# Distance tables with the four batches side by side instead of as innermost index

## The chip, the cores and the metric

The program runs on one core of one Trainium2 chip. The metric is the time of one execution in microseconds of device time, lower is better. The kernel computes a small network of two blocks on 8 sequences of 512 tokens with 256 channels, in one launch; the change touches one stage of it, the first attention.

## The reference

Of the reference only the first attention matters here. It is an attention with 16 heads of 16 channels whose scores have two more terms, which depend on the distance between query and key:

```python
scores = jnp.einsum('bhqd,bhkd->bhqk', q, k) / scale
pos_k = (rel_embeddings @ Wk + bk).reshape(2 * ATT_SPAN, nH, d)      # 128 rows of distance buckets
c2p_att = jnp.einsum('bhqd,hpd->bhqp', q, pos_k)
c2p = jnp.take_along_axis(c2p_att, c2p_pos, axis=-1)                 # c2p_pos depends on q - k only
p2c_att = jnp.einsum('bhkd,hpd->bhkp', k, pos_k)
p2c = jnp.swapaxes(jnp.take_along_axis(p2c_att, p2c_pos, axis=-1), -1, -2)
scores = scores + (c2p + p2c) / scale
probs = jax.nn.softmax(scores, axis=-1)
ctx = jnp.einsum('bhqk,bhkd->bhqd', probs, v)
```

The bucket of a distance stops to change far from the diagonal, so that a row of c2p or p2c varies only in a band around the diagonal and is constant on either side of it.

## The kernel before

**Units.** The stage works in 128 units (`UNITS`): 16 heads, two groups of four batches each (`HB = 4`), and four tiles of 128 rows (`TPB = 4`, the tile is `t`). A unit is one tile of 128 query rows of one head, for four batches; inside a unit `j` counts the batches. `each_step` writes 16 units (`BODY`) into the body of a hardware loop, so the loop turns once every 16 units.

**Distance tables.** For each unit TensorE makes two tables in PSUM, of up to 320 columns (`TABLE`) per batch: table a from the queries (`table_a`, line 679) and table b from the keys (`table_b`, line 692). ScalarE copies all four batches of table a to `a_stage` (line 789); VectorE copies batches 0 and 2 of table b and ScalarE batches 1 and 3 to `b_stage` (`copy_b`, line 767). SyncE writes both stages to DRAM (`c2p_d`, line 591, and `p2c_d`, line 598). To turn "column is a distance" into "column is a key", the table is then read back with a skew: each row of DRAM is read from one element further left than the row above it. `read_skewed` (line 559) does that in four DMAs of 32 rows for each table and unit, into `c2p` (two buffers) and `p2c` (four, one per tile). GpSimd fills the constant columns beside the band (`fill`, line 629) from the table's end columns (`copy_ends`, line 655).

**Scores.** TensorE adds q times k and the transposed `p2c` in PSUM (`scores`, lines 706, 708, 711; `p2c` is the stationary operand, which is loaded as weights). VectorE adds `c2p`, takes the minimum of the negated row and writes `probs` (line 816), ScalarE takes the exponential (line 773), TensorE transposes (line 721), VectorE copies (line 825), and TensorE multiplies by v (line 734).

**Order.** Nothing is scheduled by a program: each engine's order is that of the code. In step i SyncE waits until the scores of unit i - 1 are made, issues the four reads of p2c for unit i + 2, the four reads of c2p for unit i + 1, every four units the loads of the next group of q and k (three DMAs of 384 KB), then the write of table a of unit i + 3 and the write of table b of unit i + 4. All of these go through one DMA queue in the order of issue. On TensorE the order within batch j is scores(j), table a(j) of unit i + 3, transposes(j) of unit i - 1, table b(j) of unit i + 4; after j = 1 the product with v of unit i - 2. The single bank of table b makes TensorE wait at `table_b` until the copy of the batch before has left it.

**Layout before.** All stage buffers, DRAM tables and read tiles have the batch as innermost index, for example `a_stage[P, 2, TABLE, HB]`. A copy of one batch therefore writes every fourth float (a step of 16 bytes), VectorE's read of `c2p[:, slot, :, j]` and TensorE's weight load from `p2c` have the same step, and a row of the skewed read is one run of up to 288 x 4 floats, 4608 bytes.

Of the kernel before, what the change touches and what calls it, by code (L numbers as in the profile page):

```python
# [14 lines left out]
P = 128  # L15
# [42 lines left out]
def build(nc, a, out, taps=None):  # L58
# [8 lines left out]
    with whole:  # L67
# [33 lines left out]
        c2p_d = dram("c2p_d", [4, P, TABLE, B // 2], F32)  # L101
        p2c_d = dram("p2c_d", [4, P, TABLE, B // 2], F32)
# [349 lines left out]
        def table_cols(t):  # L452

            return (ROWS, TABLE) if t == 0 else (0, TABLE - ROWS) if t == TPB - 1 else (0, TABLE)

# [23 lines left out]
        with ExitStack() as st:  # L479
# [58 lines left out]
            with nc.Block() as block:  # L538
                @block.sync
                def _(sp):  # L540
# [13 lines left out]
                    def read_skewed(table_d, slot, t, dest, left, done):  # L554
                        for g in range(P // ROWS):
                            j0, j1 = varied(t, g)
                            skew = bass.AP(table_d.tensor, ((slot * P + ROWS * g) * TABLE + ROWS - 1 - ROWS * g + j0) * HB,
                                           [[(TABLE - 1) * HB, ROWS], [1, (j1 - j0) * HB]])
                            sp.dma_start(dest[g * ROWS:(g + 1) * ROWS, j0 + left:j1 + left, :].rearrange("p n b -> p (n b)"),
                                         skew).then_inc(done, 16)  # L560

                    def step(i, w):
# [25 lines left out]
                        if is_unit(ia, wa):  # L588
                            sp.wait_ge(a_copied, HB * (BODY * ia + wa) + HB)
                            x0, x1 = table_cols(wa % TPB)  # L590
                            sp.dma_start(c2p_d[wa % 4, :, x0:x1, :].rearrange("p n b -> p (n b)"),
                                         a_stage[:, wa % 2, x0:x1, :].rearrange("p n b -> p (n b)")).then_inc(a_written[wa % 2], 16)
                        if is_unit(ib, wb):
# [3 lines left out]
                            x0, x1 = table_cols(wb % TPB)  # L597
                            sp.dma_start(p2c_d[wb % 4, :, x0:x1, :].rearrange("p n b -> p (n b)"),
                                         b_stage[:, wb % 2, x0:x1, :].rearrange("p n b -> p (n b)")).then_inc(b_written[wb % 2], 16)
# [16 lines left out]
                def _(pool):  # L616
# [3 lines left out]
                    def step(i, w):  # L620
# [7 lines left out]
                        def fill(dest, ends_of, side, c0, c1):  # L628
                            return pool.tensor_copy(dest[:, c0:c1, :], ends_of[:, side, :].unsqueeze(1).broadcast_to(  # L629
                                [P, c1 - c0, HB]))  # L630
# [1447 lines left out]
```

## Time and profile before

| | |
|---|---|
| time before | 2948.34 us, median of 3 runs (2947.35 to 2954.58) |
| the profiled execution | 2920.05 us; its span 2918.4 us |
| the stage of the change | about 292 us to 1517 us of the span, 128 units |
| busy in the span | TensorE 1966.0 us, VectorE 1921.8 us, ScalarE 1234.3 us, GpSimd 939.9 us |
| DMA in the span | 492.63 MB, 208344 packets |

The profile gives for each engine the time in which it is busy, for each group of instructions its count, its mean time and what ended the idle time before it, and for the DMA engines how much of the time of the core's 16 engines packets were under way, with the rate in GB/s. The profiled execution took 1.65 us more than its span, and 28 us less than the median of the runs without a profile; sums are made against the profiled one, and differences are carried over to the median.

### The profile page before, as it was taken

How to read it: one execution, taken by the hardware profiler on the slowest of the kernel's cores; microseconds unless marked ns; L12 is line 12 of the kernel's file. 1: busy time of each engine (PE TensorE's matmuls, PEld its weight loads, DVE VectorE, ACT ScalarE, POOL GpSimd, SP SyncE). 2: the span in 40 equal slices, each digit the busy share in tenths (PEclk: the TensorE clock that was granted, in tenths of full speed). 3: DMA queues.
4: the chain of work that ended last, by engine and by line, in shares of the span. 5: the costliest groups of instructions: out<-in, count | busy, mean ns of one | idle time of the engine just before them, and what ended most of it. 6: DMA issues, size and time to landing. Idle time of an engine off the chain costs nothing. (4 is left out here: it accounts for less than half of the span.)

```text
span 2918.4 us, 47884 instructions
## 1 busy us (share of the span) xinstructions
PE 1966.0 (67%) x13524; PEld 1442.7 (49%) x13525; DVE 1921.8 (66%) x4329; ACT 1234.3 (42%) x2141; POOL 939.9 (32%) x1177
## 2 busy tenths in 40 slices
PE   4452677777777777777763888867613515999963
PEld 2231466555565655566552656644312502888631
DVE  5652688777787878788874666618774775444454
ACT  2332666666666666666640232224300115333200
POOL 3222222222222222222222221114774001555576
PEclk8776799999999999899986999988756555999986
DMA  4666988888888989889964121000000141444644
GB/s 136 210 204 179 292 274 284 269 275 276 265 287 273 288 271 291 267 273 289 294 184 110 43 58 29 0 20 0 0 0 2 59 165 40 154 155 151 126 131 124
DMA packets 208344, 492.63 MB, mean 169 GB/s; under 512 B 39169, under 2 KB 104353, under 8 KB 208129
## 3 DMA queue, kind: packets, MB, share of 16 engines
q1 hardware_dynamic: 179392, 420.25, 45.5%
q0 software_dynamic: 24576, 57.11, 7.9%
q10 hardware_dynamic: 4160, 12.58, 1.1%
q8 instruction: 112, 1.84, 0.3%
q14 instruction: 104, 0.84, 0.1%
HBM read 248.45 MB, written 241.30 MB: 168 GB/s over the span
## 5 line engine op out<-in xcount | busy, mean ns | idle before, releaser
L816 DVE CUSTOM_DVE_ANT_0 probs<-bank,c2p 128x512 f32<-128x512 f32 x512 | 551.5, 1077 | 231.8 <-PE bank L711 154.5
L789 ACT COPY a_stage<-bank 128x320 f32<-128x320 f32 (+1 forms) x512 | 364.5, 712 | 275.2 <-PE bank L679 269.2
L773 ACT ACTIVATE probs<-probs,neg_max 128x512 f32<-128x512 f32 x512 | 363.6, 710 | 22.5 <-DVE neg_max L816 22.0
L692 PE MATMUL bank<-tab,k 96*128 96x320 bf16 (+1 forms) x512 | 160.8, 314 | 286.1 <-DVE b_stage L767 227.8
L825 DVE COPY probsT<-bank 128x512 f32<-128x512 f32 x512 | 351.6, 687 | 2.5 <-PE bank L721 2.5
L721 PE MATMUL bank<-ident,probs 128*128 128x128 f32 x2048 | 326.5, 284 | 4.1 <-ACT probs L773 3.9
L721 PEld LDWEIGHTS bank<-ident,probs 128*128 128x128 f32 x2048 | 261.4, 148 | 18.4 <-issue 6.2
L711 PE MATMUL bank<-ident,p2c 128*128 128x128 f32 x1280 | 263.9, 307 | 0.0
L2017 POOL DMA_INDIRECT p_x_tile<-y_d,p_token x160 | 152.5, 953 | 328.2 <-POOLq L1708 208.2
L655 POOL COPY end_c2p<-a_stage 128x4 f32<-128x4 f32 (+1 forms) x128 | 24.1, 188 | 721.3 <-ACT a_stage L789 571.6
L767 ACT COPY b_stage<-bank 128x288 f32<-128x288 f32 (+1 forms) x256 | 186.3, 728 | 151.9 <-PE bank L692 150.9
L692 PEld LDWEIGHTS bank<-tab,k 96*128 96x128 bf16 x512 | 50.8, 99 | 353.3 <-DVE b_stage L767 287.7
L706 PE MATMUL bank<-k,q 96*128 96x384 bf16 (+1 forms) x512 | 162.8, 318 | 76.3 <-DMA p2c<-p2c_d 46.7
L711 PEld LDWEIGHTS bank<-ident,p2c 128*128 128x128 f32 x1280 | 199.5, 208 | 24.3 <-issue 5.6
L767 DVE COPY b_stage<-bank 128x288 f32<-128x288 f32 (+1 forms) x256 | 177.4, 693 | 47.9 <-PE bank L692 47.9
L629 POOL COPY c2p<-end_c2p 128x1408 f32<-128x1408 f32 (+2 forms) x192 | 175.4, 933 | 7.2 <-DVE neg_max L816 7.2
L1883 PE MATMUL bank<-p_w_all,p_xT 128*128 x640 | 170.7, 390 | 1.0 <-issue 0.9
L1212 POOL TENSOR_TENSOR p_pv<-p_v,p_score 128x1024 f32<-128x1024 f32 (+1 forms) x32 | 144.0, 4532 | 69.3 <-DVE p_attn L1390 48.4
L679 PE MATMUL bank<-tab,q 96*128 96x320 bf16 (+1 forms) x512 | 160.5, 314 | 1.5 <-ACT a_stage L789 0.8
L734 PE MATMUL bank<-probsT,v_h 128*32 128x128 f32 x4096 | 154.8, 297 | 0.8 <-DVE probsT L825 0.8
L1960 DVE TENSOR_TENSOR p_h<-bank,p_e_silu 128x128 f32<-128x128 f32 x160 | 46.7, 292 | 150.5 <-ACT p_e_silu L1942 150.5
L2026 POOL DMA_INDIRECT p_w_all<-o_sorted_d,p_slot x128 | 122.9, 960 | 52.4 <-issue 35.7
(252 smaller groups left out, 3931.3 us busy)
## 6 DMA issues: line engine op xcount, KB each, us to landing
p2c_d<-b_stage SPq DMA_DIRECT2D x64, 640.0 KB, 3.6
c2p_d<-a_stage SPq DMA_DIRECT2D x64, 640.0 KB, 3.4
p2c_d<-b_stage SPq DMA_DIRECT2D x64, 576.0 KB, 7.8
c2p_d<-a_stage SPq DMA_DIRECT2D x64, 576.0 KB, 5.8
p2c<-p2c_d SPq DMA_DIRECT2D x256, 144.0 KB
c2p<-c2p_d SPq DMA_DIRECT2D x256, 144.0 KB, 5.9
o_sorted_d<-p_o_pair SPq DMA_DIRECT2D x80, 256.0 KB, 2.3
q_stack_d<-p_parts SPq DMA_DIRECT2D x96, 128.0 KB
```

The source lines that it names most:

```text
L629: return pool.tensor_copy(dest[:, c0:c1, :], ends_of[:, side, :].unsqueeze(1).broadcast_to([P, c1 - c0, HB]))
L679: pe.matmul(bank[A_BANK][:, x0:x1], q6[:, g, 0, j * S + t * P:j * S + (t + 1) * P], tab6[:, w // 8, 0, x0:x1], start=True, stop=True).then ...
L692: pe.matmul(bank[B_BANK][:, x0:x1], k6[:, g, j * S + t * P:j * S + (t + 1) * P], tab6[:, w // 8, 1, x0:x1], start=True, stop=True).then_in ...
L706: pe.matmul(sc[:, near], q6[:, g, 0, own], k6[:, g, j * S + lo * P:j * S + (hi + 1) * P], start=True, stop=False, skip_group_check=True)
L711: last = pe.matmul(sc[:, kt * P:(kt + 1) * P], p2c[:, kt, (t - kt + 1) * P:(t - kt + 2) * P, j], ident[:], start=False, stop=kt == hi, is_ ...
L721: last = pe.transpose(bank[T_BANKS[j % 2]][:, kt * P:(kt + 1) * P], probs[:, w % 2, j, kt * P:(kt + 1) * P], ident[:])
L767: copy(b_stage[:, w % 2, x0:x1, j], bank[B_BANK][:, x0:x1]).then_inc(copied, 1)
L773: act.activation(probs[:, w % 2, j, :], probs[:, w % 2, j, :], ACT.Exp, bias=neg_max[:, w % 2, j:j + 1], scale=-1.0).then_inc(exp_done, 1)
L789: act.copy(a_stage[:, wa % 2, x0:x1, j], bank[A_BANK][:, x0:x1]).then_inc(a_copied, 1)
L816: dve.tensor_tensor_reduce(probs[:, w % 2, j, :], bank[S_BANKS[(HB * w + j) % 3]][:], c2p[:, w % 2, :, j], -SCALE, LOWEST, ALU.add, ALU.mi ...
L825: dve.tensor_copy(probsT[:, wp % 2, j], bank[T_BANKS[j % 2]][:].rearrange("p (k q) -> p k q", k=TPB)).then_inc(probsT_copied, 1)
L1883: last = pe.matmul(bank[GU_BANKS[w % 2]][:, 0:2 * INNER], xT[:, w % 2, c, :], weights(of_round[w], 2 * c * INNER, 2 * (c + 1) * INNER), st ...
```

## The change

The batch moves from innermost to second index in the two stage buffers, in both DRAM tables and in both read tiles. With it the columns 0 to 31 and 288 to 319, which the first and the last tile of a sequence did not make, copy or write, are now made, copied and written for all tiles (`table_cols` is gone), because the written block would otherwise not be one run per partition.

```diff
-        c2p_d = dram("c2p_d", [4, P, TABLE, B // 2], F32)
-        p2c_d = dram("p2c_d", [4, P, TABLE, B // 2], F32)
+        c2p_d = dram("c2p_d", [4, P, B // 2, TABLE], F32)
+        p2c_d = dram("p2c_d", [4, P, B // 2, TABLE], F32)
...
-        def table_cols(t):
-
-            return (ROWS, TABLE) if t == 0 else (0, TABLE - ROWS) if t == TPB - 1 else (0, TABLE)
...
-            a_stage = sb(st, "a_stage", [P, 2, TABLE, HB])
-            b_stage = sb(st, "b_stage", [P, 2, TABLE, HB])
-            c2p = sb(st, "c2p", [P, 2, S, HB])
+            a_stage = sb(st, "a_stage", [P, 2, HB, TABLE])
+            b_stage = sb(st, "b_stage", [P, 2, HB, TABLE])
+            c2p = sb(st, "c2p", [P, 2, HB, S])
...
-            p2c = sb(st, "p2c", [P, TPB, NEAR, HB])
+            p2c = sb(st, "p2c", [P, TPB, HB, NEAR])
...
-                            skew = bass.AP(table_d.tensor, ((slot * P + ROWS * g) * TABLE + ROWS - 1 - ROWS * g + j0) * HB,
-                                           [[(TABLE - 1) * HB, ROWS], [1, (j1 - j0) * HB]])
-                            sp.dma_start(dest[g * ROWS:(g + 1) * ROWS, j0 + left:j1 + left, :].rearrange("p n b -> p (n b)"),
-                                         skew).then_inc(done, 16)
+                            skew = bass.AP(table_d.tensor, (slot * P + ROWS * g) * HB * TABLE + ROWS - 1 - ROWS * g + j0,
+                                           [[HB * TABLE - 1, ROWS], [TABLE, HB], [1, j1 - j0]])
+                            sp.dma_start(dest[g * ROWS:(g + 1) * ROWS, :, j0 + left:j1 + left], skew).then_inc(done, 16)
...
-                            x0, x1 = table_cols(wa % TPB)
-                            sp.dma_start(c2p_d[wa % 4, :, x0:x1, :].rearrange("p n b -> p (n b)"),
-                                         a_stage[:, wa % 2, x0:x1, :].rearrange("p n b -> p (n b)")).then_inc(a_written[wa % 2], 16)
+                            sp.dma_start(c2p_d[wa % 4], a_stage[:, wa % 2]).then_inc(a_written[wa % 2], 16)
...
-                    copy(b_stage[:, w % 2, x0:x1, j], bank[B_BANK][:, x0:x1]).then_inc(copied, 1)
+                    copy(b_stage[:, w % 2, j, :], bank[B_BANK][:, 0:TABLE]).then_inc(copied, 1)
...
-                                act.copy(a_stage[:, wa % 2, x0:x1, j], bank[A_BANK][:, x0:x1]).then_inc(a_copied, 1)
+                                act.copy(a_stage[:, wa % 2, j, :], bank[A_BANK][:, 0:TABLE]).then_inc(a_copied, 1)
...
-                                    probs[:, w % 2, j, :], bank[S_BANKS[(HB * w + j) % 3]][:], c2p[:, w % 2, :, j],
+                                    probs[:, w % 2, j, :], bank[S_BANKS[(HB * w + j) % 3]][:], c2p[:, w % 2, j, :],
```

No instruction is added, removed or moved; the counts per engine stay, only shapes change. On SyncE's queue in the loop's body, the reads of p2c for tile 1 or 2, the reads of c2p for tile 3, and the writes around them stand before as

```order
L559 DMA p2c<-p2c_d 32x1152 x4
L559 DMA c2p<-c2p_d 32x640
L559 DMA c2p<-c2p_d 32x768
L559 DMA c2p<-c2p_d 32x896
L559 DMA c2p<-c2p_d 32x1024
L591 DMA c2p_d<-a_stage 128x1280
L598 DMA p2c_d<-b_stage 128x1152
```

and after the change as

```order
L555 DMA p2c<-p2c_d 32x4x288 x4
L555 DMA c2p<-c2p_d 32x4x160
L555 DMA c2p<-c2p_d 32x4x192
L555 DMA c2p<-c2p_d 32x4x224
L555 DMA c2p<-c2p_d 32x4x256
L585 DMA c2p_d<-a_stage 128x1280
L590 DMA p2c_d<-b_stage 128x1280
```

A row of a skewed read is now four runs of up to 288 floats instead of one run of up to 1152; a write is still one run of 1280 floats per partition, for all tiles.

## Rows read from the trace of the kernel before

**Rows 1.** The whole stage in one window: columns, then busy time of each engine
```profile
core 0: us, PE busy (x) PEld busy (x) DVE busy (x) ACT busy (x) POOL busy (x), PEclk, DMA share, GB/s
300.00:1500.00 1200.00, 888.42 (x9296) 711.71 (x9296) 962.36 (x1763) 795.49 (x1289) 310.92 (x646) 0.93 0.88 278
```

**Rows 2.** The instructions on probs: line 816, times, first and last start
```profile
L816 DVE CUSTOM_DVE_ANT_0 probs<-bank,c2p x512: 1005/1079/1180, 306.0 to 1508.2; 128x512 f32<-128x512 f32 x171
```

**Rows 3.** Waits from 300 to 1500 us: who waited for whom, us, times, longest
```profile
PE bank L692 <- DVE b_stage L767: 224.9, 227, 2.8
DVE probs L816 <- PE bank L711: 154.5, 140, 5.3
DVE probs L816 <- DMA c2p<-c2p_d: 69.7, 51, 5.3
PE bank L706 <- DMA p2c<-p2c_d: 46.7, 37, 3.1
PE bank L706 <- issue: 27.3, 9, 5.3
```

**Rows 4.** DMA from 700 to 740 us in 40 slices of 1 us: busy tenths, rate
```profile
DMA  9999999999999700008999899899999999999899
GB/s 376 423 402 310 252 229 235 373 417 413 402 318 237 182 22 0 0 0 324 389 404 299 247 256 230 213 401 400 397 313 258 238 221 215 274 262 262 221 362 414
```

**Rows 5.** SyncE's DMA issues between 708 and 722 us: start, us, issue
```profile
708.41 1.73 SPq L559 DMA_DIRECT2D c2p<-c2p_d  x4
717.40 0.34 SPq L591 DMA_DIRECT2D c2p_d<-a_stage  x1
718.61 0.34 SPq L598 DMA_DIRECT2D p2c_d<-b_stage  x1
719.82 2.48 SPq L559 DMA_DIRECT2D p2c<-p2c_d  x4
```

**Rows 6.** DMA issues of the tables: KB each, median us to landing
```profile
c2p_d<-a_stage SPq DMA_DIRECT2D x64, 576.0 KB, 5.8
c2p<-c2p_d SPq DMA_DIRECT2D x256, 144.0 KB, 5.9
```

**Rows 7.** The page's groups: busy us, mean ns of one, idle before
```profile
L816 DVE CUSTOM_DVE_ANT_0 probs<-bank,c2p 128x512 f32<-128x512 f32 x512 | 551.5, 1077 | 231.8 <-PE bank L711 154.5
L789 ACT COPY a_stage<-bank 128x320 f32<-128x320 f32 (+1 forms) x512 | 364.5, 712 | 275.2 <-PE bank L679 269.2
L767 DVE COPY b_stage<-bank 128x288 f32<-128x288 f32 (+1 forms) x256 | 177.4, 693 | 47.9 <-PE bank L692 47.9
L825 DVE COPY probsT<-bank 128x512 f32<-128x512 f32 x512 | 351.6, 687 | 2.5 <-PE bank L721 2.5
```

**Rows 8.** Groups by shape outside the stage, same columns
```profile
L1972 DVE COPY p_o_pair<-bank 128x256 f32<-128x256 f32 x160 | 66.7, 417 | 1.1 <-PE bank L1895 0.8
L1937 ACT COPY p_xT<-bank 128x256 f32<-128x256 f32 x160 | 59.5, 372 | 88.7 <-PE bank L1876 88.5
L1307 ACT COPY p_qk<-bank 128x512 f32<-128x512 f32 x32 | 18.7, 585 | 51.5 <-PE bank L1248 49.1 <-DVE p_score L1366 2.4
L1052 DVE TENSOR_TENSOR p_o<-bank,p_n_bo 128x512 f32<-128x512 f32 x16 | 11.1, 692 | 44.4 <-PE bank L961 44.4
L1596 DVE TENSOR_TENSOR p_picked<-p_hit,p_rank_e 128x4096 f32<-128x4096 f32 x1 | 7.1, 7102 | 0.0
L1574 DVE TENSOR_TENSOR p_picked<-p_hit,p_score 128x4096 f32<-128x4096 f32 x1 | 4.4, 4399 | 0.0
```

**Rows 9.** DMA from 3 to 4 us, input rows of 1 KB read from DRAM
```profile
DMA packets 367, 0.37 MB, mean 373 GB/s; under 512 B 3, under 2 KB 367, under 8 KB 367
```

**Rows 10.** SyncE's issue of a DMA, ns, min/median/max: table reads, input reads, a 3-level write
```profile
L559 SPq DMA_DIRECT2D c2p<-c2p_d x512: 302/421/1778, 301.0 to 1499.2; - x171
L903 SPq DMA_DIRECT2D p_x<-in_x x8: 387/414/1106, 1536.6 to 1775.6; - x8
L220 SPq DMA_DIRECT2D q_stack_d<-p_parts x96: 603/625/1816, 48.7 to 251.8; - x96
```

More of the change, by code:

```diff
@@ L596, in step @@
                             sp.wait_ge(b_copied_act, 2 * (BODY * ib + wb) + 2)
[L597 to L599 removed]
+                            sp.dma_start(p2c_d[wb % 4], b_stage[:, wb % 2]).then_inc(b_written[wb % 2], 16)
                         ic, wc = ahead(i, w, -2)
@@ L628, in fill @@
                         def fill(dest, ends_of, side, c0, c1):
-                            return pool.tensor_copy(dest[:, c0:c1, :], ends_of[:, side, :].unsqueeze(1).broadcast_to(
-                                [P, c1 - c0, HB]))
+                            return pool.tensor_copy(dest[:, :, c0:c1], ends_of[:, side, :].unsqueeze(2).broadcast_to(
+                                [P, HB, c1 - c0]))
                         if is_unit(i2, w2):
@@ L654, in copy_ends @@
                             apart(pool)
-                            pool.tensor_copy(ends_of[:, w % 4, ends(t), :], stage[:, w % 2, end_cols(t), :]
-                                             ).then_inc(copied, 1)
+                            pool.tensor_copy(ends_of[:, w % 4, ends(t), :].rearrange("p s b -> p b s"),
+                                             stage[:, w % 2, :, end_cols(t)]).then_inc(copied, 1)
                         if is_unit(ia, wa):
@@ L677, in table_a @@
                         wait_count(pe, a_copied, HB * m + j)
-                        x0, x1 = table_cols(t)
-                        pe.matmul(bank[A_BANK][:, x0:x1], q6[:, g, 0, j * S + t * P:j * S + (t + 1) * P],
-                                  tab6[:, w // 8, 0, x0:x1], start=True, stop=True).then_inc(a_made, 1)
+                        pe.matmul(bank[A_BANK][:, 0:TABLE], q6[:, g, 0, j * S + t * P:j * S + (t + 1) * P],
+                                  tab6[:, w // 8, 0, :], start=True, stop=True).then_inc(a_made, 1)
                     def table_b(i, w, j):
@@ L690, in table_b @@
                             wait_count(pe, b_copied_act, 2 * m + j // 2)
-                        x0, x1 = table_cols(t)
-                        pe.matmul(bank[B_BANK][:, x0:x1], k6[:, g, j * S + t * P:j * S + (t + 1) * P],
-                                  tab6[:, w // 8, 1, x0:x1], start=True, stop=True).then_inc(b_made, 1)
+                        pe.matmul(bank[B_BANK][:, 0:TABLE], k6[:, g, j * S + t * P:j * S + (t + 1) * P],
+                                  tab6[:, w // 8, 1, :], start=True, stop=True).then_inc(b_made, 1)
                     def scores(i, w, j):
@@ L710, in scores @@
                         for kt in range(lo, hi + 1):
-                            last = pe.matmul(sc[:, kt * P:(kt + 1) * P], p2c[:, kt, (t - kt + 1) * P:(t - kt + 2) * P, j],
+                            last = pe.matmul(sc[:, kt * P:(kt + 1) * P], p2c[:, kt, j, (t - kt + 1) * P:(t - kt + 2) * P],
                                              ident[:], start=False, stop=kt == hi, is_transpose=True,
```

2 lines of the change are left out of this document (removed).

## The prediction

> **What bounds the kernel now.** I first read the stage as one window [rows 1]. From 300 to 1500 us VectorE is busy 962.36 of 1200 us (80%), TensorE 888.42, ScalarE 795.49, and the DMA engines have packets under way 0.88 of the time. No engine is full; the DMA share is the highest number in the row. The instructions on probs give the length of a unit: 512 instructions of line 816 start from 306.0 to 1508.2 us, so four of them, one unit, take 4 x 1202.2 / 511 = 9.41 us [rows 2]. With [rows 1], in a unit VectorE works 0.802 x 9.41 = 7.55 us, TensorE 6.97 us, ScalarE 6.24 us, the DMA engines 0.88 x 9.41 = 8.28 us; they are idle for 1.13 us.
>
> Then the waits [rows 3]. Two kinds take turns. TensorE waits 224.9 us for VectorE's copy of table b, and VectorE 154.5 us for TensorE's scores: the two hand work to and fro, and a faster VectorE shortens both. But VectorE also waits 69.7 us for the skewed read of c2p, at 51 of 128 units, and TensorE 46.7 us for that of p2c at 37. So in a good part of the units the read is late, not the arithmetic.
>
> Last the DMA by microsecond [rows 4]. The reader is to see three levels. Near 400 to 420 GB/s the tables are written; at 213 to 258 GB/s, with the same 9 tenths busy, the skewed reads run; and for 715 to 717 us nothing runs. The issues tell which is which [rows 5]: the reads issued at 708.41 us are through by 714; the write of table a is issued at 717.40 us; with the write of table b it makes the slices of 324 to 404; the reads from 719.82 us make those of 299 down to 213. The hole from 714 to 718 us is the time in which SyncE waits until ScalarE has copied table a of that unit. So the DMA queue has work for 8.28 us per unit, and idles when the arithmetic is late with a copy; the arithmetic idles when a read lands late behind the loads of q and k. A read of c2p takes 5.9 us from issue to landing [rows 6].
>
> **What the change gives the engines.** VectorE's line 816 reads c2p with a step of 16 bytes and takes 1077 ns [rows 7]. What such a step costs is shown outside the stage: of two instructions of the same operation and size, the one whose second operand has a large step takes 7102 ns and the one without 4399 ns for 4096 elements, 0.66 ns per element [rows 8]. For 512 that is 338 ns, so line 816 falls to about 739 ns. A plain tensor_tensor of 512 from PSUM takes 692 ns [rows 8], so both estimates agree. If line 816's length were its own and not the step's, this gain would be 0; the 692 ns make me take the 338.
>
> The copy of table b takes 693 ns on VectorE [rows 7]. Copies without a step take 417 ns for 256 columns [rows 8] and 687 ns for 512 [rows 7], 1.055 ns per column, so 484 ns for 320 columns, which all tiles now have: 209 ns less. Per unit VectorE saves 4 x 338 + 2 x 209 = 1770 ns, and has 5.78 us of work. ScalarE's copies take 712 ns [rows 7]; without a step 372 ns for 256 and 585 ns for 512 [rows 8] give 425 ns for 320. Six per unit save 1.7 us. ScalarE was never waited for long; this matters since SyncE's write of table a stands behind it. TensorE's weight loads from p2c lose their step too; they lie beside matmuls, and I count 0. Its table matmuls get 32 more columns in half of the units; TensorE's 6.97 us leave 2.4 us of cover, and without it this would be a tenth of those matmuls in those units.
>
> The Trainium skill, SBUF — State Buffer, Specifications, says that SBUF is read in lines of 16 bytes and that an access which goes to a new line each time pays. A step of four floats is just that, and the rows above agree.
>
> GpSimd's fills write as many elements as before and its copies of end columns are tiny; I take 0 for both, and they are covered by the issue of the p2c reads ahead of the c2p reads.
>
> **What it costs the DMA queue.** Writes: tiles 0 and 3 wrote 576 KB per table [rows 6] and now write 128 x 1280 floats, 640 KB, on average 64 KB more per unit; at about 400 GB/s [rows 4] this is 0.16 us. Reads: same bytes, but each of the 256 rows of a unit's eight reads comes in 4 runs of at most 1152 bytes, 768 more pieces. The trace has no such read. The nearest row is that of input rows of 1 KB read from DRAM: 373 GB/s, 43.9 ns for a piece on one of 16 engines [rows 9]. At the best rate of large pieces, 423 GB/s [rows 4], the same bytes take 38.7 ns, so a piece has 5.2 ns of its own, and 768 of them on 16 engines cost 0.25 us per unit. That is the upper bound. The lower bound is 0, and I lean to it: the skewed reads now run at 213 to 258 GB/s, far below the 373 that pieces of 1 KB reach, so something other than the piece limits them, and the piece's overhead can hide under it. A gain I exclude, since bytes, rows and partitions stay. I take 0.10 us. SyncE's issue of one read has a median of 421 ns; a load with four runs per partition has 414, a write with three levels and a register in its address 625 [rows 10]. I take no change; at 625 it would be 8 x 0.204 = 1.6 us more per unit on a queue that issues for about 4.2 us of 9.4.
>
> The Trainium skill, SBUF — State Buffer, Door 1, says that 32 partitions reach only 8 of the 16 ports, 218 GB/s; each skewed read fills 32 partitions, and the slices of 213 to 258 agree with that. The Trainium skill, DMA: Bandwidth & Descriptors, How a descriptor splits into AXI transactions, speaks against the change: a piece that does not start on a multiple of 256 bytes fetches up to 256 bytes more. By that page, as an estimate, 768 pieces fetch up to 197 KB more, which at 240 GB/s would be 0.8 us per unit.
>
> **The sum.** The arithmetic can now do a unit in less than the queue: VectorE 5.78 us, TensorE 6.97 us with waits around it. So the unit is what the queue needs, plus what idling stays. Need: 8.28 + 0.16 + 0.10 = 8.54 us. Idle before: 1.13 us. Of it a part does not go: at the turn of the hardware loop TensorE stands up to 5.3 us, 27.3 us in all [rows 3], 0.21 us per unit. Of the other 0.92 us I keep a third, 0.30, for the latency between a read's landing and the next write. The unit is 8.54 + 0.21 + 0.30 = 9.05 us, 0.36 us less; times 128 units 46 us. Against the profiled 2920.05 us that gives 2874; carried to the median of the runs, 2948 - 46 = 2902 us.
>
> The forecast's own range: with nothing for pieces and no idle but that of the loop turns, the unit is 8.28 + 0.16 + 0.21 = 8.65 us, 97 us less, 2851. With 0.25 us for pieces and half of the 0.92 us of idle kept it is 8.28 + 0.16 + 0.25 + 0.21 + 0.46 = 9.36 us, 6 us less, 2942.
>
> **Rivals.**
> Slower: the queue's need grows by more than its idling shrinks. The place is the skewed reads. It decides from the point where growth plus remaining idle passes 1.13 us. If pieces cost 0.25 us and the arithmetic, since it has only two buffers for c2p, can't issue its writes earlier, the unit is 8.28 + 0.41 + 1.13 = 9.82 us, 52 us more, 3001. For it speaks that the queue is already at 0.88; against it that the hole from 714 to 718 us [rows 4, 5] ends with the issue of a write that had waited for a copy, and that copy gets faster. Chance 0.12. By the Trainium skill's rule on pieces off 256 bytes, named above, the same rival would come by another road: 8.28 + 0.16 + 0.8 + 0.51 = 9.75 us, an estimate of 2992 us; no row here shows that cost, and it shares the 0.12.
>
> No change: either line 816 keeps its 1077 ns (VectorE then works 7.13 us, most of the idle stays, and the unit is about 9.4 us) or cost and gain cancel. 2939 to 2957. Chance 0.12.
>
> Much faster: the busy share of the DMA engines is no need, but packets that wait and would go faster if asked earlier. Then the hand-over between VectorE and TensorE was the bound, and the unit falls to TensorE's 6.97 us and some 0.6 us of waits, 7.6 us: 232 us less, 2716; halfway, 2830. For it speaks that 154.5 + 224.9 us of waits hang on VectorE. Against it: 16 engines are busy at 213 to 258 GB/s [rows 4], and c2p lands late at 51 units already. Chance 0.10.
>
> The forecast itself has 0.66.
>
> **How the numbers follow.** Faster by over 0.3% (about what a measurement of this kernel can tell from no change, 9 us): the forecast and the last rival, 0.76. Within 0.3%: 0.12. Slower: 0.12. The range that holds 8 in 10 covers the forecast and no change, and a little of each side: 2845 to 2960.
>
> **What would show it.** Line 816 near 740 ns and the copies of tables near 484 (VectorE) and 425 ns (ScalarE) would show the first step. VectorE's wait for c2p should grow from 69.7 us at more than 51 units, its wait for TensorE and TensorE's for the b copy should shrink, and the DMA share of the window should rise to 0.93 or more. The slices of the reads should stay at 213 to 258 GB/s; if they fall below 200, the pieces cost what I leaned against, and I am wrong on the slow side. If the share falls with a shorter unit, I am wrong on the fast side.

## The result, and the profile after

The changed kernel takes 2924.62 us (median of 6 runs, 2918.56 to 2938.00), the kernel before 2947.85 us in the same sets of runs. The ratio is 0.9926, with an interval of 0.9898 to 0.9954: 22 us faster, where 46 were forecast. The time lies in the forecast's range, and the gain is a little under half of the forecast gain.

The length of the stage and of a unit, in the trace of the changed kernel (line 803 is line 816 of before; times are minimum, median and maximum in ns, then first and last start in us):

```profile
L803 DVE CUSTOM_DVE_ANT_0 probs<-bank,c2p x512: 679/691/694, 301.4 to 1483.8; 128x512 f32<-128x512 f32 x171
```

A unit is 4 x 1182.4 / 511 = 9.256 us where it was 9.41 [rows 2]: 0.155 us less, 20 us over 128 units. In these two traces the stage also starts 4.6 us earlier, and it ends 24.4 us earlier; the start is not the change's doing, for in a second trace of the kernel before (e16) it lies at 302.9 us. The medians differ by 23 us, about what the stage gained. The last section says why the profiled times of the two kernels (2920.05 and 2926.19 us) do not show it.

The page's groups after, as in [rows 7] (busy us, mean ns, idle before):

```profile
L803 DVE CUSTOM_DVE_ANT_0 probs<-bank,c2p 128x512 f32<-128x512 f32 x512 | 351.5, 687 | 423.4 <-PE bank L700 215.3
L776 ACT COPY a_stage<-bank 128x320 f32<-128x320 f32 x512 | 217.8, 425 | 490.0 <-PE bank L669 444.0
L755 DVE COPY b_stage<-bank 128x320 f32<-128x320 f32 x256 | 123.2, 481 | 47.4 <-PE bank L681 47.4
```

The engine terms came as forecast or better: 687 ns (forecast 739), 425 (425) and 481 (484). The window of [rows 1] after the change:

```profile
300.00:1500.00 1200.00, 916.22 (x9443) 734.19 (x9442) 752.29 (x1785) 644.03 (x1294) 314.63 (x650) 0.88 0.93 285
```

VectorE fell from 962 to 752 us and ScalarE from 795 to 644, and the share of the DMA engines rose from 0.88 to 0.93. TensorE's mean granted clock fell from 0.93 to 0.88: of its two levels, 1.2 and 2.4 GHz, it had the lower one for 24% of the window instead of 14%. Its work per unit rose from 6.97 to 7.07 us. The waits, as in [rows 3]:

```profile
DVE probs L803 <- PE bank L700: 215.3, 172, 7.5
DVE probs L803 <- DMA c2p<-c2p_d: 188.3, 65, 7.3
PE bank L695 <- DMA p2c<-p2c_d: 138.2, 52, 5.0
PE bank L681 <- DVE b_stage L755: 79.5, 129, 2.9
PE bank L695 <- issue: 36.8, 10, 7.2
```

The time that VectorE no longer works has become waiting. Waits for the two reads grew from 116.4 us (69.7 + 46.7) to 326.5 us (188.3 + 138.2). TensorE's wait for the b copy fell from 224.9 to 79.5 us, but VectorE's wait for the scores rose from 154.5 to 215.3 us. TensorE's longer wait for p2c explains little of that: laid side by side in the trace, the two waits overlap in 13 us. For most of it TensorE was at work, and VectorE, whose operations are shorter, stood waiting for it. The DMA slices from 700 to 740 us, as in [rows 4]:

```profile
DMA  9815999999999999999999999999999999999955
GB/s 266 192 31 246 410 400 248 303 251 230 251 345 423 420 326 249 232 243 240 215 266 242 250 214 391 415 421 348 245 241 249 337 408 430 387 316 252 238 125 231
```

The holes are nearly gone. The levels are the old ones: writes at 400 to 430 GB/s, reads at 214 to 266. The read of c2p lands later after its issue, 6.8 us against 5.9 [rows 6]:

```profile
c2p<-c2p_d SPq DMA_DIRECT2D x256, 144.0 KB, 6.8
```

### The profile page after: what moved, and what is told of

Its sections match the earlier page's. It is cut to its first block and busy times, and to the rows that moved or that the text cites. A ratio compares the mean times of both kernels' runs of the same rounds, so it can differ in the third digit from the quotient of the medians.

```text
span 2924.5 us, 47884 instructions
## 1 busy us (share of the span) xinstructions
PE 1980.1 (68%) x13524; PEld 1454.9 (50%) x13525; DVE 1695.2 (58%) x4329; ACT 1072.3 (37%) x2141; POOL 941.1 (32%) x1177
## 5 line engine op out<-in xcount | busy, mean ns | idle before, releaser
L803 DVE CUSTOM_DVE_ANT_0 probs<-bank,c2p 128x512 f32<-128x512 f32 x512 | 351.5, 687 | 423.4 <-PE bank L700 215.3
L776 ACT COPY a_stage<-bank 128x320 f32<-128x320 f32 x512 | 217.8, 425 | 490.0 <-PE bank L669 444.0
L710 PE MATMUL bank<-ident,probs 128*128 128x128 f32 x2048 | 346.9, 297 | 1.4 <-ACT probs L761 1.2
L710 PEld LDWEIGHTS bank<-ident,probs 128*128 128x128 f32 x2048 | 288.6, 156 | 16.5 <-issue 2.6
L681 PE MATMUL bank<-tab,k 96*128 96x320 bf16 x512 | 171.5, 335 | 146.8 <-DVE b_stage L755 82.3
L700 PEld LDWEIGHTS bank<-ident,p2c 128*128 128x128 f32 x1280 | 163.2, 156 | 26.6 <-issue 7.6
L669 PE MATMUL bank<-tab,q 96*128 96x320 bf16 x512 | 171.8, 336 | 0.0
L695 PEld LDWEIGHTS bank<-k,q 96*128 96x128 bf16 x512 | 52.4, 102 | 226.1 <-issue 183.2
L755 DVE COPY b_stage<-bank 128x320 f32<-128x320 f32 x256 | 123.2, 481 | 47.4 <-PE bank L681 47.4
L697 PE MATMUL bank<-k,q 96*128 96x128 bf16 (+1 forms) x512 | 136.0, 266 | 0.0
```

The lines of the kernel that those rows point to most:

```text
L669: pe.matmul(bank[A_BANK][:, 0:TABLE], q6[:, g, 0, j * S + t * P:j * S + (t + 1) * P], tab6[:, w // 8, 0, :], start=True, stop=True).then_i ...
L681: pe.matmul(bank[B_BANK][:, 0:TABLE], k6[:, g, j * S + t * P:j * S + (t + 1) * P], tab6[:, w // 8, 1, :], start=True, stop=True).then_inc( ...
L695: pe.matmul(sc[:, near], q6[:, g, 0, own], k6[:, g, j * S + lo * P:j * S + (hi + 1) * P], start=True, stop=False, skip_group_check=True)
L700: last = pe.matmul(sc[:, kt * P:(kt + 1) * P], p2c[:, kt, j, (t - kt + 1) * P:(t - kt + 2) * P], ident[:], start=False, stop=kt == hi, is_ ...
L710: last = pe.transpose(bank[T_BANKS[j % 2]][:, kt * P:(kt + 1) * P], probs[:, w % 2, j, kt * P:(kt + 1) * P], ident[:])
L776: act.copy(a_stage[:, wa % 2, j, :], bank[A_BANK][:, 0:TABLE]).then_inc(a_copied, 1)
```

## The experiments

The unit of each kernel is worked out as above, from the first and the last start in its trace. Ratios are to the kernel before, run on the same chip. A unit comes from one profiled execution, and that execution can lie off the median of its kernel: 21 us below for e10, 6 to 7 below for e9 and e11, 11 above for e6 and e8, 13 above for e18. In a unit this is 0.05 to 0.16 us, so a difference of units of 0.1 us counts only where the ratios say the same.

| | edit | unit us | ratio (interval) |
|---|---|---|---|
| | before / before again (e16) | 9.41 / 9.42 | 1 |
| | changed kernel | 9.26 | 0.993 (0.990 to 0.995) |
| e1 | before, contiguous engine operations | 8.95 | 0.981 (0.978 to 0.983) |
| e2 | before, reads cut, negative step | 9.68 | 1.013 (1.010 to 1.015) |
| e3 | e1 and e2 | 9.30 | 0.996 (0.994 to 0.998) |
| e4 | changed, writes at 288 columns in 4 runs | 9.25 | 0.994 (0.992 to 0.996) |
| e5 | e1, reads cut, positive step | 9.05 | 0.982 (0.979 to 0.985) |
| e6 | changed, row starts on 16 bytes | 9.32 | 0.993 (0.990 to 0.995) |
| e7 | e1, row starts on any 4 bytes | 8.99 | 0.981 (0.978 to 0.984) |
| e8 | changed, reads of distant halves in turn | 9.12 | 0.982 (0.980 to 0.985) |
| e9 | e1, 320 columns everywhere | 9.16 | 0.990 (0.987 to 0.993) |
| e10 | changed, reads in pairs 1, 0, 3, 2 | 9.13 | 0.993 (0.991 to 0.996) |
| e11 | changed, e8 and e13 together | 8.84 | 0.976 (0.973 to 0.979) |
| e12 | before, reads as in e8 | 9.27 | 0.992 (0.990 to 0.994) |
| e13 | changed, 288 columns in one run | 9.07 | 0.984 (0.983 to 0.986) |
| e14 | changed, reads half as long | 8.50 | 0.961 (0.959 to 0.963) |
| e15 | before, reads half as long | 8.84 | 0.975 (0.973 to 0.977) |
| e17 | changed, loads in three steps | 9.17 | 0.988 (0.985 to 0.991) |
| e18 | e11 and e17 | 8.94 | 0.974 (0.970 to 0.978) |

**e1, the engines alone.** Copies, line 816 and the weight loads walk flat rows; all DMAs are those of before.

```diff
-                    copy(b_stage[:, w % 2, x0:x1, j], bank[B_BANK][:, x0:x1]).then_inc(copied, 1)
+                    flat = b_stage[:, w % 2].rearrange("p n b -> p (n b)")
+                    at = HB * x0 + j * (x1 - x0)
+                    copy(flat[:, at:at + x1 - x0], bank[B_BANK][:, x0:x1]).then_inc(copied, 1)
```

> The kernel before, with its tiles, DMAs and column counts, but every engine operation on the stage buffers and on the read tile walks them contiguously instead of at a step of four. It reads and writes the tables in another order, so the values of the distance terms are not the reference's. It asks what the shorter engine times alone are worth. Theory (the queues' work bounds the unit): DVE's weighted sum near 690 ns instead of 1077, the unit 8.28 of DMA need + 0.21 of loop turns + 0.3 to 0.5 of kept idle = 8.8 to 9.0 us instead of 9.41, so 50 to 80 us less than before, about 2880. Rival (the hand-over between engines bounds it): 7.6 us per unit, over 200 us less. Second rival (engine times were never on the path): the unit stays at 9.4 and the time at 2948.

The instructions of line 816, which is line 825 here, and the window from 300 to 1400 us, which lies wholly in the stage:

```profile
L825 DVE CUSTOM_DVE_ANT_0 probs<-bank,c2p x512: 678/690/693, 299.6 to 1442.6; 128x512 f32<-128x512 f32 x171
```

```profile
300.00:1400.00 1100.00, 865.67 (x8927) 694.71 (x8925) 705.47 (x1698) 603.78 (x1244) 297.49 (x620) 0.88 0.94 293
```

62 us less and a unit of 8.95 us: the first theory. The shorter operations are worth 0.46 us of a unit, and the other parts of the change take two thirds of that back. (In e1 the granted clock is 0.88 too, so it did not fall by those other parts.)

**e2 and e3, the reads in four pieces.**

```diff
-                                            [[(TABLE - 1) * HB, ROWS], [1, (j1 - j0) * HB]])
+                                            [[(TABLE - 1) * HB, ROWS], [-n, HB], [1, n]])
```

The read begins 3 * n floats on, and its target steps back in the same way.

> The kernel before, in which each skewed read of a table comes in four pieces a quarter as long, with the same bytes and the same layout; all that is computed stays. It asks what the smaller pieces of the change cost by themselves. Theory: 768 extra pieces per unit cost 0 to 0.25 us, so the unit is 9.4 to 9.66 us and the time 0 to 32 us more. Rival: the pieces cost much more, 0.8 us per unit and 100 us in all, and are what ate the gain of the change. Second rival: the DMA need isn't what bounds, and the time stays within 5 us.

> The two edits together: contiguous engine operations and reads in four pieces, without the 32 extra columns per batch that the change writes. It reads and writes the tables in another order, so the values of the distance terms are not the reference's. Theory: the unit of the first experiment plus 0.1 to 0.25 us for the pieces, 8.95 to 9.2 us, which is the changed kernel's 9.26 less up to 0.16 for the narrower writes; time 2900 to 2925. Rival (pieces are cheap, the writes are the loss): the same time as the first experiment within 5 us.

Both lost, a little more than the theories allow: 0.27 us of a unit on before, 0.36 on e1. But the edit brought something that the change does not have. SyncE's issue of a read in e2 (min, median, max ns):

```profile
L563 SPq DMA_DIRECT2D c2p<-c2p_d x512: 560/601/1752, 300.1 to 1533.1; - x171
```

601 ns, where before has 421 [rows 10] and the changed kernel 432. Eight reads per unit make 1.4 us more on SyncE's queue. So neither run prices the pieces, and e5 does it again with a positive step.

**e4, the writes narrower.**

```diff
-                            sp.dma_start(c2p_d[wa % 4], a_stage[:, wa % 2]).then_inc(a_written[wa % 2], 16)
+                            x0, x1 = table_cols(wa % TPB)
+                            sp.dma_start(c2p_d[wa % 4, :, :, x0:x1], a_stage[:, wa % 2, :, x0:x1]).then_inc(a_written[wa % 2], 16)
```

> The changed kernel, with the first and the last stage buffer of a row written out at 288 columns of each batch instead of 320 (four runs of 1152 bytes per partition instead of one of 5120); all that is computed stays. It asks what the wider writes cost. Theory: they are 0.16 us per unit, so the unit falls from 9.26 to 9.1 us and the time by 20 us, to about 2904. Rival (a write costs by its count of pieces and not by its bytes): the time stays at 2924 or rises by a few us.

No gain. The rival seemed to hold, that columns cost nothing. But this edit too trades one thing for another: it cuts each of these writes into four runs of 1152 bytes. e9 and e13 price the columns without that, but they change more than the write: the columns are also made and copied, or not.

**e5, e6 and e7: count and place of the pieces.**

e5, on e1:

```diff
-                                            [[(TABLE - 1) * HB, ROWS], [1, (j1 - j0) * HB]])
+                                            [[(TABLE - 1) * HB, ROWS], [j1 - j0 - 4, HB], [1, j1 - j0]])
```

e6, on the changed kernel (all reads also begin at column 124, so that the rows stay inside the table):

```diff
-                                           [[HB * TABLE - 1, ROWS], [TABLE, HB], [1, j1 - j0]])
+                                           [[HB * TABLE - 4, ROWS], [TABLE, HB], [1, j1 - j0]])
```

e7, on e1:

```diff
-                                            [[(TABLE - 1) * HB, ROWS], [1, (j1 - j0) * HB]])
+                                            [[(TABLE - 1) * HB + 1, ROWS], [1, (j1 - j0) * HB]])
```

> The first experiment's kernel (contiguous engine operations, values of the distance terms not the reference's), with each skewed read in four pieces that overlap by four floats at their source, so that a piece keeps its place on 16 bytes and SP issues the read at a positive step. Experiments 2 and 3 cut the reads with a negative step, and SP took 601 ns to issue one instead of 421, which may be their loss. Theory A (the count of pieces costs, on the queues): SP's issue near 430 ns, and still the unit is 8.95 + 0.30 = 9.25 us as in the changed kernel, the time 38 us over the first experiment, 2924. Theory B (the loss of experiments 2 and 3 was SP's issue time, and what the changed kernel lost was the place of its row starts): the time of the first experiment within 8 us, 2886.

> The changed kernel, in which the rows of a skewed read begin four floats apart instead of one, all on multiples of 16 bytes as in the kernel before; counts and sizes of pieces stay. It reads other columns of the tables, so the values of the distance terms are not the reference's. Theory A (the count of pieces costs): no change, 2924 within 8 us. Theory B (row starts at any 4 bytes cost): the unit falls from 9.26 towards 8.95 us and the time to about 2886.

> The first experiment's kernel with long pieces of 4608 bytes as there, whose rows begin one float off from row to row, at any multiple of 4 bytes (values of the distance terms not the reference's). Theory A (count of pieces): the first experiment's time, 2886 within 8 us. Theory B (place of row starts): a loss; a quarter as many starts as in the changed kernel, so 8 to 38 us over it.

SyncE's issue of a c2p read in e5:

```profile
L559 SPq DMA_DIRECT2D c2p<-c2p_d x512: 302/432/1966, 297.0 to 1449.7; - x171
```

Its median is 432 ns, as in the changed kernel. The stage of e5 ends 15 us after that of e1:

```profile
L825 DVE CUSTOM_DVE_ANT_0 probs<-bank,c2p x512: 679/688/694, 302.5 to 1458.0; 128x512 f32<-128x512 f32 x171
```

The 768 extra pieces of a unit cost 0.10 us of it by these two profiles; the ratios (0.982 against 0.981) give 0.03 us, and do not tell it from nothing. Theory A of e5, 38 us for the pieces, falls. Where the rows start, on 16 bytes or on any 4, makes no difference that can be seen: e6 equals the changed kernel by its ratio, e7 equals e1. So the second half of theory B, that the change lost by its row starts, falls too; its first half, that the issue time was the loss of e2 and e3, is left standing, though the direction of their step differs too. Most of the 0.31 us between e1 and the changed kernel had to be something else.

**e9 and e13, the 32 columns.** e9 lets all of e1's tables be 320 wide, and e13 makes the changed kernel's first and last table of a row 288 wide, packed side by side.

e9, on e1:

```diff
-            return (ROWS, TABLE) if t == 0 else (0, TABLE - ROWS) if t == TPB - 1 else (0, TABLE)
+            return (0, TABLE)
```

e13, on the changed kernel:

```diff
+        def packed(rows, t):
+            x0, x1 = table_cols(t)
+            return rows[:, 0:HB * (x1 - x0)]
...
-                            sp.dma_start(c2p_d[wa % 4], a_stage[:, wa % 2]).then_inc(a_written[wa % 2], 16)
+                            sp.dma_start(packed(c2p_d[wa % 4], wa % TPB), packed(a_stage[:, wa % 2], wa % TPB)).then_inc(a_written[wa % 2], 16)
```

> The first experiment's kernel (contiguous engine operations, long pieces, values of the distance terms not the reference's), with all 320 columns of each batch computed, copied and written for every stage buffer, as the changed kernel does. It adds the columns alone. Theory (the columns cost what the forecast's write term says, 0.16 us per unit): the unit goes from 8.95 to 9.11 us, and with the 0.10 that cutting the reads was measured at this makes 9.2 of the changed kernel's 9.26; time 20 us over the first experiment, 2906. Rival (the columns cost nothing, as the fourth experiment suggests, and where the pieces of a read land is what costs): the first experiment's time within 8 us.

> The changed kernel with the batches of the first and the last table of a row side by side at 288 columns instead of 320, computed, copied and written as such in one piece of 4608 bytes per partition; the order of the reads is the changed kernel's. All that is computed stays. Theory (the 32 columns cost 0.22 us per unit, as between experiments 1 and 9): the unit falls from 9.26 to 9.04 us, the time by 28 us, ratio to the kernel before 0.983. Rival (the columns cost nothing, as experiment 4 seems to say): ratio 0.993.

The stage of e9:

```profile
L825 DVE CUSTOM_DVE_ANT_0 probs<-bank,c2p x512: 679/691/694, 300.3 to 1471.0; 128x512 f32<-128x512 f32 x171
```

The stage of e13 (its line 822 is line 803 of the changed kernel):

```profile
L822 DVE CUSTOM_DVE_ANT_0 probs<-bank,c2p x512: 678/690/693, 301.4 to 1459.7; 128x512 f32<-128x512 f32 x171
```

The columns cost 9.16 - 8.95 = 0.22 us (with unrounded units) on e1, and taking them out of the changed kernel gives back 9.26 - 9.07 = 0.19 us, with ratios 0.009 apart, some 25 us. These are columns that TensorE makes, the engines copy and SyncE writes; how much of the price is the written bytes, neither run separates. e4 took away the written bytes alone and had no gain. That its four runs ate one is likely but not shown: its queues have a share of 0.97, against 0.95 in the changed kernel and in e13, though they move 7 GB/s less than the changed kernel's.

**e8, e10 and e12, the order of a table's four reads.**

```diff
-                        for g in range(P // ROWS):
+                        for g in (0, 2, 1, 3):
```

(e10 has (1, 0, 3, 2).)

> The changed kernel, in which SP issues the four reads of a table for partitions 0 to 31, 64 to 95, 32 to 63, 96 to 127 instead of in rising order; all that is computed stays. Theory (while two reads are in the queues together they are bound by the part of the memory that 32 or 64 neighbouring partitions reach; 213 to 258 GB/s in the read phases): reads of distant partitions run side by side, the reads' phase shortens by a tenth or more, the unit falls by 0.2 to 0.5 us and the time by 25 to 60 us. Rival (the level comes from the order in which each queue works off its pieces, or from the pieces themselves): 2924 within 8 us.

> The changed kernel, in which SP issues the four reads of a table for partitions 32 to 63, 0 to 31, 96 to 127, 64 to 95: another order than the rising one, but neighbours still follow each other in the same half. All that is computed stays. Theory (experiment 8's gain came from reads of different halves in the queues together): no gain, 2924 within 8 us, unit 9.26. Rival (any order that breaks the rising one gains, by the sizes of the reads or the part of DRAM they start in): about 2900, unit 9.12.

> The kernel before with the order of experiment 8 alone (partitions 0 to 31, 64 to 95, 32 to 63, 96 to 127). All that is computed stays. Theory (the read phases bound the kernel before too): a gain of the same size, 0.1 to 0.3 us of the unit's 9.41, 15 to 35 us, about 2925. Rival (before, the engines' waits keep most of it, since its idle share was 0.12 against 0.07): less than 8 us.

Order 0, 2, 1, 3 takes 1.0% off the changed kernel and 0.8% off the kernel before; order 1, 0, 3, 2 takes nothing by its ratio, 0.993. (Its unit of 9.13 is that of a run 21 us below the median.) So it is not a new order as such that gains, but one in which reads of partitions 64 apart follow each other. The queues' work shows it as well: from 300 to 1500 us the share is 0.89 in e8 and 0.94 in e10, with units of the same length and the same bytes. The Trainium skill, SBUF — State Buffer, Door 1, has a reason: partitions 32 apart share the DMA ports, partitions 64 apart have others. The trace agrees in the landing of a c2p read, 5.5 us against 6.8:

```profile
c2p<-c2p_d SPq DMA_DIRECT2D x240, 144.0 KB, 5.5
```

e11 puts e8 and e13 together. Its theory was that the gains add, 2881 to 2901 us where the kernel before takes 2948, a ratio of 0.977 to 0.984. It has 0.976, so they do.

**e14 and e15, half of each read.**

```diff
                             j0, j1 = varied(t, g)
+                            j1 = (j0 + j1) // 2
```

> The changed kernel with only the first half of the columns of each skewed read (pieces of 320 to 576 bytes, as many as before; the rest of the read tiles is zero, so the values of the distance terms are not the reference's). Theory (the queues' work bounds the unit): 8.6 us of work per unit falls by some 2 us, to 6.4 to 6.6, and the unit falls to the hand-over bound of the prediction's last rival, 7.6 us, or with kept idle of 0.65 even to 7.1; over 190 us less than the changed kernel, below 2740. Rival (the unit is held by the engines' chain and the queues only look full): 9.0 to 9.3 us, less than 30 us gained.

> The kernel before with only the first half of the columns of each skewed read (the rest of the read tiles is zero, so the values of the distance terms are not the reference's). Theory (the kernel before is bound by the queues with engines close behind): the unit falls to where the longer engine operations bound it, by DVE's 962 of 1200 us of work 7.6 us at the least and with its idle time by the chain near 8.4 us; 2820 or less. What it is over the run before (with the changed kernel's shorter operations) is what these are worth with the queues out of the way: 0.7 us per unit or more, against the 0.46 of experiment 1. Rival: both fall to the same unit.

The unit falls, but to 8.50 us: not to the theory's 7.1 or 7.6, and below the rival's 9.0 to 9.3. Four units in turn of e14, each from the first instruction of line 806 (803 of the changed kernel) to that of the next unit; columns as in [rows 1]:

```profile
644.85:652.09 7.24, 5.26 (x67) 4.39 (x68) 5.82 (x14) 4.23 (x10) 1.74 (x5) 1.00 0.85 266
652.09:663.56 11.47, 6.71 (x73) 5.20 (x72) 5.81 (x14) 4.79 (x10) 4.01 (x7) 0.83 0.98 323
663.56:671.56 8.00, 7.89 (x79) 6.54 (x78) 6.01 (x15) 5.05 (x11) 0.27 (x2) 0.82 0.52 163
671.56:678.84 7.28, 6.41 (x76) 5.16 (x75) 5.81 (x16) 5.12 (x11) 3.34 (x8) 1.00 0.84 277
```

Three of four units take 7.2 to 8.0 us with the queues at 0.52 to 0.85. The other one takes 11.5 with the queues full: before it, from 649.8 to 652.2 us, SyncE has issued the next group of k and q, and here the next head's tables too, ahead of the writes and reads that follow. In the changed kernel:

```profile
676.05:684.33 8.28, 7.32 (x84) 5.91 (x81) 5.82 (x15) 5.86 (x12) 1.96 (x5) 1.00 1.04 280
684.33:696.99 12.66, 7.60 (x73) 6.08 (x73) 5.91 (x15) 5.10 (x11) 2.96 (x6) 0.87 1.05 321
696.99:703.74 6.75, 5.55 (x70) 4.50 (x69) 5.73 (x14) 4.16 (x10) 0.26 (x2) 1.00 0.81 264
703.74:712.89 9.15, 6.39 (x76) 5.15 (x75) 5.81 (x16) 5.10 (x11) 4.97 (x10) 1.00 1.03 319
```

(A share counts the packets that began in the stretch with all their time, so in a single unit it can pass 1.) Both bounds are there, in different units, and a mean unit hides it. The whole stage says the same. With the units sorted into their four kinds, in the order of these lines, and each kind's mean length taken from the starts on probs (units 5 to 124 of the 128), the kernel before has 9.37, 10.50, 8.80 and 9.29 us, the changed kernel 8.80, 11.15, 7.66 and 9.78, and e14 8.05, 10.32, 7.70 and 8.29; the second trace of before (e16) differs from the first by 0.12 at most, that of e6 from the changed kernel's by 0.25. So the change shortened two kinds of units, by 0.57 and 1.14 us, and lengthened the other two, by 0.65 and 0.49: two thirds of the gain came back as longer units, and these are the kinds whose queues are full above.

e15 is 0.34 us over e14, and not the 0.7 or more expected. This is the price of the whole layout, its pieces and columns included, and not that of the operations alone: with half of each read the change is worth 0.34 us of a unit, with whole reads 0.155.

**e17 and e18, the loads spread.**

```diff
-                        if w % TPB == 0 and is_unit(i, w) and is_unit(*ahead(i, w, 2 * TPB)):
-                            load_group(2 * i + w // 8 + 1, (w // TPB) % 2, (w // TPB + 2) % 4)
+                        if w % TPB < 3 and is_unit(i, w) and is_unit(*ahead(i, w - w % TPB, 2 * TPB)):
+                            load_group(2 * i + w // 8 + 1, (w // TPB) % 2, (w // TPB + 2) % 4, [w % TPB])
```

> The changed kernel, in which SP issues the three loads of the next k and q group in three steps (k in the first unit of a row, q in the second, the far q in the third) instead of all three in the first. Bytes and all that is computed stay. Theory (the unit with the loads holds 2 to 3 us that the others can't take back): the unit of 11.5 us falls to 9.5 to 10.5 while two others rise by 0.3 to 0.6, the mean falls by 0.1 to 0.4 us and the time by 15 to 50 us, ratio to before 0.975 to 0.988. Rival (the queues' work sets the mean whatever its order): ratio 0.993 as the changed kernel's.

> Experiment 11's kernel (tables at 288 columns side by side, reads issued by distant halves) with the loads in three steps as in experiment 17. All that is computed stays. Theory: as much below experiment 11's ratio of 0.976 as experiment 17 is below the changed kernel's 0.993, 0.960 to 0.972. Rival: 0.976.

Four units in turn of e17; the load of k is issued ahead of the second, at 675.2 us, and that of q in it, at 683.3 us:

```profile
671.34:679.50 8.16, 7.54 (x86) 6.23 (x84) 5.82 (x15) 6.10 (x13) 1.85 (x5) 1.00 1.04 265
679.50:689.85 10.35, 8.26 (x78) 6.49 (x76) 6.00 (x15) 5.49 (x12) 2.55 (x6) 0.84 1.06 312
689.85:698.77 8.92, 7.16 (x70) 5.98 (x71) 6.00 (x14) 4.29 (x9) 1.30 (x4) 0.81 1.05 301
698.77:707.05 8.28, 6.07 (x73) 4.85 (x72) 5.82 (x14) 4.96 (x11) 3.80 (x9) 1.00 1.01 328
```

The long unit shrank and its neighbour grew, from 6.75 to 8.92 us (over the stage, in the mean, 11.15 to 9.41 and 7.66 to 8.65); the queues are now full in all four. The mean fell by 0.09 us. The ratio, 0.988, is at the edge of the theory's window, its interval overlaps that of the changed kernel, and e18 is not told apart from e11. So the loads in one place are not what holds most of the time. That with them spread the sum of the queues' work does fits the full queues, but was not tried by itself. e11 and e18 beat both kernels; e11's ratio, 0.976, with its interval, is the surer of the two.

**e16, the kernel before again.**

> The kernel before, unchanged, for its profile. The stage of the tables ended at 1508 us in the first profile, and everything after it took 1410 us. If the chip sets the latter, it is 1410 where the median of before is near 2921 and 1437 to 1443 where it is near 2948, while the stage ends at 1505 to 1511 on both. If the first profile was only a lucky run, the later code takes about 1440 here whatever the median.

Line 816 in its trace:

```profile
L816 DVE CUSTOM_DVE_ANT_0 probs<-bank,c2p x512: 1005/1079/1156, 302.9 to 1506.7; 128x512 f32<-128x512 f32 x171
```

Its span is 2954.6 us, on a chip where the kernel before has a median of 2951.28: the stage ends as in [rows 2], and the rest takes 1448 us, not 1410.

## Why the prediction came out at half

- **That the DMA queues bound the changed kernel, and arithmetic that gets shorter shows only in part:** right. VectorE's busy time per unit fell by 1.75 us (7.55 to 0.627 x 9.256 = 5.80), and the unit by 0.155.
- **The engine durations:** right for the copies; line 816 was priced 52 ns too long, since the step cost it 0.76 ns per element and not 0.66. The sum does not use it, since it takes the unit to be what the queues need.
- **"Need: 8.28 + 0.16 + 0.10 = 8.54 us":** this is the step that failed. It takes what the queues did before, 8.28 us, as a fixed amount that other work is added to. Windows that lie wholly in the stage, of the changed kernel, e9, e5, e4 and e14 in turn:

```profile
300.00:1400.00 1100.00, 844.74 (x8596) 676.43 (x8595) 686.74 (x1638) 594.43 (x1202) 288.65 (x600) 0.87 0.95 290
300.00:1400.00 1100.00, 847.07 (x8660) 675.85 (x8659) 690.51 (x1651) 599.44 (x1211) 290.13 (x604) 0.88 0.93 293
300.00:1400.00 1100.00, 852.53 (x8800) 683.89 (x8800) 695.87 (x1674) 597.73 (x1228) 292.92 (x610) 0.88 0.95 289
300.00:1400.00 1100.00, 834.83 (x8592) 667.75 (x8590) 685.50 (x1637) 595.94 (x1202) 289.00 (x600) 0.89 0.97 283
300.00:1380.00 1080.00, 864.30 (x9274) 693.31 (x9277) 734.86 (x1760) 635.64 (x1285) 310.49 (x641) 0.92 0.79 256
```

The changed kernel's queues work 0.95 x 9.26 = 8.79 us of a unit, 0.25 more than the sum has, and idle for 0.46 us, where the sum kept 0.51. So the 0.21 us by which the unit was missed lie in the need. With the bytes and the pieces of before, e1 already has 0.94 x 8.95 = 8.41 us for what made 8.28. On top of it the cut reads add 0.95 x 9.05 - 8.41 = 0.18 us and the columns 0.93 x 9.16 - 8.41 = 0.11 (shares are rounded, which leaves 0.05 us in each of these).
- **"Of the other 0.92 us I keep a third, 0.30":** a guess without a row behind it, which came out near by luck: with the loop turns 0.51 us, and e1 idles for 0.54, the changed kernel for 0.46. The deeper fault is the model under both terms, that a mean unit is a need plus idle time. Work taken off the queues is not exchanged one for one: e14 took 2.1 us of it off a unit (0.95 x 9.26 less 0.79 x 8.50) and shortened it by 0.75, since units in which the queues are full stand beside units in which the hand-overs between engines end last.
- **The wider writes, 0.16 us:** the columns cost 0.22 (e9) and 0.19 (e13), but with the matmuls and the copies that go with them, which the sum leaves out. What the bytes cost is not shown. At the mean rate of the stage, 285 GB/s, the 64 KB would be 0.23 us instead of the 0.16 at a write's best rate; this is an estimate, and e4, which writes fewer bytes, had no gain.
- **The pieces, 0.10 us:** right for the unit (e5: 0.10 by the profiles, 0.03 by the ratios, give or take 0.08), and that is partly luck, for the queues' work grew by 0.18 us and the unit took over only a part. That SyncE's issue does not grow was right as well (421 to 432 ns); what a growth by 170 ns would have cost, e3 against e5 suggests: 0.26 us of a unit, though the direction of the step differs too.
- **TensorE:** its work was left at 6.97 us and is 7.07; in e1, without the wider tables, it is 7.04 at the same granted clock of 0.88. It stays below the unit, but VectorE waits for it 215.3 us. What the lower clock costs a unit no run here separates.
- **Starts of pieces off 256 bytes,** the rule of the Trainium skill, DMA: Bandwidth & Descriptors, How a descriptor splits into AXI transactions, with the prediction's estimate of 0.8 us: not seen. By e5 cutting costs 0.10 us of a unit and 0.18 us of the queues' work in all, and e6 and e7 move the starts in steps of 16 and 4 bytes without effect; no run here has all starts on multiples of 256.
- **The signs named ahead:** the wait for c2p grew (188.3 us, 65 times), the wait for the b copy shrank, the share rose to 0.93, the slices kept their level. VectorE's wait for scores was to shrink and grew: with its operations shorter, it now more often waits while TensorE works.

By the runs, 9.41 - 0.46 (e1) + 0.10 (e5) + 0.22 (e9) = 9.27 us, and the changed kernel has 9.26; by the ratios of the same runs, - 0.45 + 0.03 + 0.22 = - 0.20 us against - 0.17. So these three parts leave nothing open that the runs could tell. What stays open is why the queues' share grows in e1 with equal bytes; that reads wait longer behind one another when the writes come earlier fits the landing times but was not tried by itself.

The rivals: "no change" and "slower" did not come; the hand-over bound of 7.6 us is near what the three shorter kinds of units in e14 take (8.0 us in the mean), but the kind of unit that follows the loads takes 10.3 us there.

## What to carry to other kernels

When a stage has two limits near each other, take the length of each kind of unit from the trace before pricing a gain on the mean: here one unit in four followed the loads with its queues full, two kinds of units grew while two shrank, and of the work that e14 took off the queues a third came back as time. Do not take a queue's busy time as a fixed need either: it grew by 0.13 us of a unit with the same bytes when the engines got faster. And look at which partitions the transfers in flight fill: in rising order the read phases ran at 214 to 266 GB/s, and issuing reads of partitions 64 apart in turn gained 0.8% and 1.0%, as much as the change itself or more.

## What the hardware showed unexpectedly

- **The order of the reads:** told above, 30 us (e8) and 23 us (e12) by the ratios for four numbers in a loop. The units, 0.13 and 0.14 us shorter, show less of it for e8, whose profile was of a run 11 us above the median.
- **A negative step in a DMA:** the issue on SyncE took 601 ns instead of 432 for the same number of runs (e2, e5). The two differ in more than the sign (e2 has the step on both sides), so which it is stays open.
- **Chips differ outside the stage.** In five profiles (the first of before, e9 to e12) the code behind the stage takes 1408 to 1411 us; in the other fifteen, the second of before among them, 1437 to 1448. The stage itself is alike in the one kernel that was profiled on both kinds of chip (e16). For the last four of the five the kernel before had a median of 2921.38 us on the same chip, for the others 2947 to 2954. So the first profile of before, 28 us under its median, very likely came from such a chip; its stage could be compared, its total could not.
